# Taking the products of zeros out of TensorE's queue ahead of the first expert steps

## The reference, cut to what matters

```python
x = x + wkv(w, u, layernorm(x), ctx)          # a scan over the 64 positions of each sequence
x = x + ffn(layernorm(x))                     # 32 experts, 8 chosen for each token

probs = softmax(x @ gate_w)                   # the logits: 256 -> 32 experts
w, sel = top_k(probs, 8);  w = w / sum(w)
g = xg @ w_gate;  u = xg @ w_up               # 256 -> 96, each expert
y = (silu(g) * u) @ w_down                    # 96 -> 256
out[token] += w * y
```

## Time and profile before

| | us |
|---|---|
| three timed executions | 268.12, 268.70, 270.14 |
| their median | 268.7 |
| the profiled execution's own time | 269.13 |
| its span, first to last instruction | 266.8 |
| TensorE busy in it | 243.9 (91%), 1058 instructions |
| products of zeros (L728) | 28 recorded of 29, 11.8 busy |
| mean granted TensorE clock | 0.976 of full speed |

### The profile page before, as it was taken

The page is one execution under the profiler, slowest core; times in us unless marked ns, Lnnn a source line. Parts: engine busy times, 40 slices in busy tenths (PEclk is TensorE's granted clock), DMA queues, the critical chain, the costliest instruction groups (busy, mean ns, idle before and its releaser), DMA issues.

```text
span 266.8 us, 3968 instructions
## 1 busy us (share of the span) xinstructions
PE 243.9 (91%) x1058; PEld 186.9 (70%) x1061; DVE 134.8 (51%) x342; ACT 134.3 (50%) x242; POOL 161.1 (60%) x140
## 2 busy tenths in 40 slices
PE   6636798799999999999999999999999999999993
PEld 1412486677678777778687778787878787878772
DVE  4598887339562794439643534235342332424333
ACT  2766453576366753594377635343525353435320
POOL 5118202856768565858586675858677686868610
PEclk9999879799999999999999999999999999999998
DMA  7950500006050524124050505050505060700002
GB/s 208 258 147 22 156 26 0 0 0 185 16 154 22 135 64 121 56 50 127 10 169 6 173 1 161 17 153 26 156 21 166 13 173 17 222 22 0 1 0 79
DMA packets 43359, 22.23 MB, mean 83 GB/s; under 512 B 34128, under 2 KB 43344, under 8 KB 43344
## 3 DMA queue, kind: packets, MB, share of 16 engines
q1 hardware_dynamic: 42496, 21.63, 28.1%
q10 hardware_dynamic: 848, 0.43, 0.6%
HBM read 21.01 MB, written 1.05 MB: 83 GB/s over the span
## 4 chain that ended last, share of the span: by engine, by line
PE 68%; DVE 14%; ACT 6%; issue 6%; POOL 4%; DMA 1%; DVEq 0%; POOLq 0%; ACTq 0%
PE bank L699 40%; PE bank L717 8%; PE bank L721 7%; PE bank L718 7%; DVE t_sb L1042 3%; DVE bank L911 2%; DVE inv L922 2%; POOL rstd L357 2%; DVE t_sb L1048 2%; PE bank L616 2%; PE bank L657 2%; PE bank L706 1%; ACT normed L446 1%; DMA x_sb<-in_x_dram 1%; POOL t_lo L375 1%
## 5 line engine op out<-in xcount | busy, mean ns | idle before, releaser
L375 POOL TENSOR_TENSOR t_lo<-t_sb,t_hi 128x512 fp32r<-128x512 f32 x47 | 60.8, 1294 | 75.1 <-ACT t_hi L542 75.1
L349 POOL TENSOR_TENSOR wlo<-raw,whi 128x768 fp32r<-128x768 f32 x48 | 88.5, 1847 | 6.7 <-ACT whi L505 6.5
L699 PE MATMUL bank<-h_hi,whi 128*128 128x512 f32 x192 | 80.8, 421 | 0.3 <-issue 0.3
L1042 DVE TENSOR_TENSOR t_sb<-bank,s_sb 128x512 f32<-128x512 f32 x48 | 33.1, 690 | 93.4 <-PE bank L706 45.8
L699 PE MATMUL bank<-h_lo,whi 128*128 128x512 f32 x192 | 76.7, 400 | 0.0
L699 PE MATMUL bank<-h_hi,wlo 128*128 128x512 f32 x192 | 76.2, 397 | 0.0
L542 ACT ACTIVATE t_hi<-t_sb 128x512 fp32r<-128x512 f32 x48 | 30.3, 630 | 90.9 <-DVE t_sb L1048 90.9
L505 ACT ACTIVATE whi<-raw 128x768 fp32r<-128x768 f32 x48 | 40.0, 835 | 8.6 <-PE bank L721 8.6
L699 PEld LDWEIGHTS bank<-h_hi,whi 128*128 128x128 f32 x192 | 36.9, 192 | 8.8 <-issue 0.8
L699 PEld LDWEIGHTS bank<-h_hi,wlo 128*128 128x128 f32 x192 | 36.6, 191 | 8.8
L699 PEld LDWEIGHTS bank<-h_lo,whi 128*128 128x128 f32 x192 | 36.8, 192 | 8.0
(11 more groups left out here) (120 smaller groups left out, 194.0 us busy)
## 6 DMA issues: line engine op xcount, KB each, us to landing
raw<-in_L_ffn_w_gate_dram SPq DMA_DIRECT2D x16, 384.0 KB
raw<-in_L_ffn_w_up_dram SPq DMA_DIRECT2D x16, 384.0 KB
raw<-in_L_ffn_w_down_dram SPq DMA_DIRECT2D x48, 128.0 KB
out_dram<-x SPq DMA_DIRECT2D x4, 256.0 KB, 2.5
x_sb<-in_x_dram SPq DMA_DIRECT2D x1, 512.0 KB, 7.0
ctx_tile<-in_ctx_dram SPq DMA_DIRECT2D x4, 128.0 KB, 5.2
x_sb<-in_x_dram SPq DMA_DIRECT2D x1, 256.0 KB, 3.4
ctx_sb<-in_ctx_dram SPq DMA_DIRECT2D x1, 256.0 KB, 4.6
```

Source lines behind the costliest of these rows:

```text
L349: pool.tensor_tensor(split_view(wlo, slot, part), raw_parts(slot, part), split_view(whi, slot, part).bitcast(F32), ALU.subtract).then_inc( ...
L375: pool.tensor_tensor(t_lo[k % 2][:], t_sb[:], t_hi[k % 2][:].bitcast(F32), ALU.subtract).then_inc(t_lo_ready, 1)
L699: last = nc.tensor.matmul(ps[:], up_weight(w, slot, part, k, j), h[:, k, tokens], start=(i == 0), stop=(i == len(terms) - 1))
L1042: nc.vector.tensor_tensor(t1_sb[:], w_ps[:], s_sb[:], ALU.mult).then_inc(t1_ready, 1)
```

## The change

The function `keep_clock` and its three calls go. The waits that stood around the calls stay as they are, and so does every other instruction of every queue, `start_sums` with its two products of zeros (L730 to L732) among them: those open the accumulation banks.

```diff
-            def keep_clock(count):
-
-                for i in range(count):
-                    nc.tensor.matmul(bank[7][:], zeros_bf[:, 0:P], zeros_bf[:], start=(i == 0), stop=(i == count - 1))
-
...
             pe.sem_inc(down_done, 2)
             pe.wait_ge(consts_ready, 1)
-            keep_clock(10)
             for u in (*first_units, early):
                 turn_kv(u)
             pe.wait_ge(inv_ready, 1)
-            keep_clock(7)
             turn_mixed(first_units[0])
             turn_mixed(first_units[1])
-            keep_clock(12)
             turn_h(first_units[0])
             turn_h(first_units[1])
             logits(first_routed[0])
```

## The result

| | before | changed |
|---|---|---|
| median, 20 executions each | 269.33 us | 270.16 us |
| lowest to highest | 268.03 to 270.48 | 269.46 to 271.19 |
| profiled execution, own time | 269.13 | 269.76 |
| its span | 266.8 | 268.1 |
| TensorE busy, instructions | 243.9, 1058 | 235.6, 1032 |

The ratio is 1.0039, 95% interval 1.0021 to 1.0057: by it the changed kernel is 1.05 us slower (0.57 to 1.54), while the two medians lie 0.83 us apart. That is within 1%, though the interval excludes 1. The forecast was 270.2 us.

A forecast was written before the change was run, and what follows sets the result against it. TensorE was taken to bound the kernel from the second unit's logits at 34.38 us through the first 18 expert products; 2.3 + 0 - 0.8 = +1.5 us on a median of 268.7 gave 270.2 us, range 268.4 to 272.3.

The forecast's parts named there:

- The logits at half clock: 24 logits products from 32.76 us, 0.222 us apart instead of 0.111; first expert product 2.3 us later.
- the bounds: Extra time per logits product at half clock: nothing to 0.143 us, 0.11 taken; 0 to 3.1 us in all.
- Rival B: Logits no slower at half clock, so no change: 268.7 us, or 267.9 with the dip's middle value; chance 0.17.
- The covers: Slower transposes before the logits cost 0, hidden by 0.97 and 0.34 us of slack before VectorE needs their results.
- The 18 products: First expert products after the logits: full clock again after 3.3 us as before, so 0, from -1.6 to +2.2 us.
- Rival A: Clock stays low longer, most or all 18 expert products at half clock: 272.3 to 273.2 us; chance 0.2.
- The later dip: Half clock at 49.34 to 52.76 us behind TensorE's pause, costing 1.6 us: between 0 and -1.6, middle -0.8.
- The ten products: First batch of zeros, ending at 7.07 us: nothing waits for it and the clock behind it was low anyway; 0.

The follow-up runs named there:

- the changed kernel with the filled pause: Changed kernel plus seven products of zeros ahead of the early unit's norm wait in the first turn's pause: 269.56 us, ratio 1.0023 to the kernel before.
- Filling the pause: Kernel before plus seven products of zeros ahead of the early unit's norm wait in TensorE's first-turn pause: 267.97 us, ratio 0.9943.
- the kernel with the seven products behind the wait: Kernel before plus seven more products of zeros in the first turn, run only after the early unit's norm wait: 268.67 us, ratio 0.9988.

## Why the prediction was right

The direction was right and clear of noise, and the cause is the forecast one. That the number, 270.2 us, falls on the median of 270.16 is luck. The forecast was +1.5 us on a median of three executions, 268.7; over 20 executions that median is 269.33, and the time grew by 0.83 us in the medians and 1.05 by the ratio. In the spans the growth is 1.5 us, as forecast, but there too the terms were not the forecast ones. By its steps:

- **The logits at half clock: right, and the main term.** Forecast 0.222 us each, measured 0.213; the first expert product forecast 2.3 us later, measured 1.95 (2.1 counted from when the first low part released the logits, which was 0.14 us earlier). Over the executions the term is smaller, about 1.5 us, because the clock often fell within the logits of the kernels that have the twelve. The choice between the bounds was right for the reason given, the transposes being whole instructions: the load grew by 0.141 us, the distance by 0.102. The load of this format took 333 ns in the logits, against 192 before. The page's rule for the load time (Trainium skill, "TensorE: Matmul & The Clock Gate", section "LDWEIGHTS (loading the stationary operand)"), in which no clock stands, does not hold here. Rival B falls with the logits' own distance, 0.213 us and not 0.111 in the changed kernel.
- **The covers: right.** The second transposes cost 1.13 us and ScalarE ended 0.3 us before VectorE needed it, forecast 0.34. The last part of the weights was ready at 41.7, forecast 41.8.
- **The 18 products, 0: right over the executions, too low for the profiled one.** There they took 0.87 us more, the clock rising 5.1 us after the first one and not 3.3. Rival A had this the right way and about half its price. In the changed kernel with the filled pause the same 18 took 5.60 us, so it differs between executions. On average the kernels with the twelve were no faster here.
- **The later dip, -0.8: too large over the executions.** In the profiled pair it was wholly gone (-1.6). Over the 20 executions of the changed kernel it came in about 11, which is the half that the forecast took. But the forecast let the kernel before always have it, because its profiled execution has it. Filling the pause gave 0.8 us of mean span there and 0.6 in the changed kernel, so the difference that the dip makes between the two is nearer to -0.2.
- **The ten products, "gain 0, loss 0": wrong as a general sentence.** I read one execution, in which they did not raise the clock. In others they do: of the seven profiled executions that have the ten, five ran the first transposes at full clock. The prediction also called what the chain has on TensorE there single transposes, while the chain of the kernel before has eight of them with 2.21 us:

```profile
7.72 2.21 PE bank L616 x8
```

  In an execution of the kernel with the seven products behind the wait, TensorE's first transposes and VectorE's first mix were:

```profile
2.62 4.41 PE L729 MATMUL bank<-zeros_bf 128*128 128x512 bf16 x10 [2.62 <-POOL ident L333]
7.51 0.72 PE L616 MATMUL bank<-ident,normed 128*128 128x128 f32 x4 [0.48 <-ACT normed L446]
8.29 0.74 PE L616 MATMUL bank<-ident,ctx_sb 128*128 128x128 f32 x4
```

```profile
20.59 0.68 DVE L945 TENSOR_TENSOR mixed<-bank,inv 128x504 f32<-128x504 f32 x1
```

Four transposes took 0.72 us where the earlier trace rows have 1.11, and the mix started at 20.59; in the profiled execution of the kernel before it started at 21.46, of which 0.2 us is the earlier landing of x. These transposes are on the path, so such an execution gains about 0.7 us early. It may lose it again later, and over many executions no measured difference was left. The mean recorded clock was 0.962 or less in 93 of the 102 executions of the kernel before, and never below 0.977 in the 12 of the kernel without the ten. So the profiled execution, with 0.976, seems to be a rare one in this; yet the 93 and the other nine have the same mean span, 267.0 us.

Two readings were off without weight: the trace has 36 transposes between 7.7 and 32.2 us and not 28, and products of zeros at half clock start about 0.427 us apart, where 0.445 is a batch's length, with its last product's end, shared out.

In the profiled pair the sum came out nearly exact in the span because two misses cancelled: +0.9 for the products against -0.8 more for the dip. Over the executions the terms come roughly, from few profiled ones, to 1.5 for the logits, -0.3 for the products and -0.2 for the dip, 1.0 us of the 1.5 in span. The other 0.5 us no run attributes, nor the 0.5 us that come back outside the span.

## What to carry to other kernels

Instructions that compute nothing can be worth their place where they keep TensorE's clock up for what comes next on the path, above all for short matmuls with a full weight load each, which took 0.21 instead of 0.11 us here. Here only the batch next to the work that it served counted, and a pause is filled only from ahead of the wait that makes it; the same seven products gained about 1.1 us by standing before a wait and not behind it. Before such a batch is called idle, look at the distances between starts and at several executions, since one trace shows one position of the clock's changes. Take the median that a forecast starts from out of many executions too, and keep the part outside the span apart from the instructions: three executions put it 0.6 us too low here, more than half of the effect.

## What the runs showed of the hardware

- The distance of a 128x128 load with a 32-column product of this format was 0.111 us at full and 0.213 us at half clock: nearly all of it scales with TensorE's clock.
- Ten unbroken products of 128x512, 4.4 us, were followed by full clock in one execution (four transposes 0.72 us) and by half clock in another (1.11 us); of the seven profiled executions with them, five had 0.71 to 0.73 us and two 1.10 and 1.11. What TensorE did just before did not decide this by itself.
- The granted clock in these profiles has no entry ahead of its first one and reads 1.00 there, up to 43 us in the changed kernel, while its expert products at 39 to 42 us lie 0.427 us apart.
